# Column sums of Wq by VectorE additions and one product with minus ones, and raw transposed x loaded from tile 2 on

## The reference

```python
h = layernorm(x)
q = rotate(h @ Wq); k = rotate(ctx @ Wk); v = ctx @ Wv
x = x + softmax(q k^T / 4) v @ Wo
h = layernorm(x)
scores = (h @ Wr^T) @ keys^T
gate = softmax over the 16 largest scores, 0 elsewhere
out = x + 2 * ((h @ A^T).reshape(64, 8) * gate).reshape(512) @ B^T
```

## Time and profile before

| | us |
|---|---|
| median of 3 runs | 168.08 (167.92 to 168.69) |
| profiled execution | 168.37 |
| its span in the trace | 166.7 |
| TensorE busy | 160.6 (96%) |
| VectorE busy | 135.0 (81%) |
| ScalarE busy | 95.8 (57%) |
| GpSimd busy | 87.9 (53%) |

### The profile page before, as it was taken

One profiled execution on the slowest core, in us unless ns is written; L12 is line 12 of the kernel. 1 busy time (PEld: TensorE's weight loads), 2 busy tenths in 40 slices (PEclk: granted clock), 3 DMA queues, 4 the chain that ended last, 5 costly groups with the idle time before them and its releaser, 6 DMA issues.

```text
span 166.7 us, 4195 instructions
## 1 busy us (share of the span) xinstructions
PE 160.6 (96%) x1437; PEld 128.9 (77%) x1437; DVE 135.0 (81%) x394; ACT 95.8 (57%) x216; POOL 87.9 (53%) x114
## 2 busy tenths in 40 slices
PE   7899999899999999999999999999999999999993
PEld 2557786777878787879887987979898877779883
DVE  2959895995998899699888998799886997867562
ACT  3588989899657453942678138832487254414210
POOL 6469999899889843724942098106321204411200
PEclk9999999999999999999999999999999999999999
DMA  5999961303315234415442263114410001000013
GB/s 118 403 402 387 409 198 67 132 6 120 98 32 159 49 79 110 117 46 172 114 112 66 93 163 94 49 49 144 109 64 4 4 0 65 0 6 0 0 63 126
DMA packets 12116, 18.45 MB, mean 111 GB/s; under 512 B 2496, under 2 KB 5056, under 8 KB 11840
## 3 DMA queue, kind: packets, MB, share of 16 engines
q1 hardware_dynamic: 11808, 17.93, 34.9%
q10 hardware_dynamic: 288, 0.27, 0.5%
HBM read 11.11 MB, written 2.10 MB: 79 GB/s over the span
## 4 chain that ended last, share of the span: by engine, by line
PE 81%; DVE 9%; issue 3%; DMA 3%; ACT 2%; ACTq 0%; DVEq 0%
PE ps_w L1342 12%; PE ps_w L1343 11%; PE ps_w L1347 11%; PE ps_t L1355 6%; PE ps_s L1426 4%; PE ps_w L1335 3%; PE ps_w L1337 3%; PE ps_w L1336 3%; DVE ps_s L1029 3%; DMA cT_in<-cT 3%; PE ps_t L1496 2%; PE ps_w L1559 2%; PE ps_t L1347 2%; PE ps_t L1343 2%; PE ps_t L1342 2%
## 5 line engine op out<-in xcount | busy, mean ns | idle before, releaser
L483 POOL TENSOR_TENSOR late<-late,gate 128x512 f32<-128x512 f32 x7 | 7.6, 1084 | 31.5 <-issue 15.0
L698 ACT ACTIVATE eT<-ps_s 128x512 f32<-128x512 f32 x32 | 17.0, 601 | 2.5 <-PE ps_s L1485 1.6
L1342 PE MATMUL ps_w<-am_hi,x2T_hi 128*128 128x288 f32 x48 | 13.8, 310 | 0.3 <-ACT x2T_hi L719 0.2
L468 POOL TENSOR_TENSOR oT_lo<-o_n,oT_hi 128x512 fp32r<-128x512 f32 x8 | 10.4, 1294 | 6.6 <-ACT oT_hi L706 6.6
L1343 PE MATMUL ps_w<-am_lo,x2T_hi 128*128 128x288 f32 x48 | 13.1, 296 | 0.0
L1342 PE MATMUL ps_w<-b_hi,zT_hi 128*128 128x512 f32 (+1 forms) x28 | 11.0, 398 | 0.0
L1019 DVE TENSOR_REDUCE ps_s<-ps_s 128x8 f32<-128x512 f32 x16 | 10.6, 688 | 0.3 <-PE ps_s L1426 0.2
L1029 DVE TENSOR_REDUCE ps_s<-ps_s 128x8 f32<-128x512 f32 x16 | 10.4, 692 | 0.5 <-PE ps_s L1445 0.3
L1335 PE MATMUL ps_w<-wq_hi,xT_hi 128*128 128x512 f32 x26 | 10.8, 414 | 0.0
L414 POOL TENSOR_TENSOR rstd<-ve,neg_half 128x1 f32<-128x1 f32 x8 | 4.4, 554 | 11.8 <-DVE ve L947 10.5
L1343 PE MATMUL ps_w<-b_lo,zT_hi 128*128 128x512 f32 (+1 forms) x28 | 10.4, 378 | 0.0
(11 more groups left out here) (280 smaller groups left out, 549.5 us busy)
## 6 DMA issues: line engine op xcount, KB each, us to landing
x_sb<-x SPq DMA_DIRECT2D x8, 256.0 KB, 6.2
q_stack<-qT_hi SPq DMA_DIRECT2D x32, 64.0 KB, 2.0
cT_in<-cT SPq DMA_DIRECT2D x7, 256.0 KB, 3.1
out<-res SPq DMA_DIRECT2D x7, 256.0 KB, 2.3
wq_sb<-wq SPq DMA_DIRECT2D x4, 256.0 KB, 5.1
late<-wo SPq DMA_DIRECT2D x1, 1024.0 KB, 7.5
am_sb<-aT SPq DMA_DIRECT2D x1, 1024.0 KB, 8.3
b_sb<-bT SPq DMA_DIRECT2D x1, 1024.0 KB, 6.7
```

The costliest lines, as they stand in the source:

```text
L468: pool.tensor_tensor(oT_lo[:], o_n[:].rearrange("p (b r q) -> p r b q", b=2, r=REP), oT_hi[:].bitcast(F32), ALU.subtract).then_inc(oT_lo_o ...
L698: act.activation(eT[:, c].rearrange("p b n -> p (b n)"), ps_s[:, c, :], ACT.Exp)\
L1342: pe.matmul(dst, hi(k), w_hi[:, k, cols], start=(k == 0), stop=False)
```

## The change

- DIRECT goes from 4 to 2: tiles 2 and 3 no longer are normalised and turned, their raw x is loaded. `rotate_q(2)` and `rotate_q(3)` get the additional VectorE instruction, and `deviation1(2)` and `deviation1(3)` make a `cs_q`. `x_low(2)` on VectorE reads `xT_raw` in SBUF, not PSUM; `x_low(3)` goes from VectorE to GpSimd.
- The column sums: three VectorE additions over the four chunks of Wq (`add_wq`, into `res`) and one fp32 product of a 128x128 tile of minus ones with the 128x512 result. The four loads, the four ScalarE passes and the four transposes go. `sum_columns` and `sums_out` move from the end of step 1 to `second()`.
- In `first()` on TensorE `kv_high(2)` and `kv_low(2)` stand ahead of and behind `turn_m(0)`; `kv_low(2)` stood behind the turned scores.
- In step 1 `turn_m(2)` stands between the halves of `out_low(1)`, and on VectorE `m_parts(2)`, `k_low(3)` and `residual(1)` stand ahead of `x2_low(0)` and `rotate_q(3)`.
- `statistics1(3)` on VectorE and `deviation1(3)` on GpSimd move to the end of `second()`.

```diff
-DIRECT = 4
+DIRECT = 2
...
-        sums = sb("sums", [P, DK])
+        neg_ones = sb("neg_ones", [P, P])
...
-            return (ps_t1 if t < FIRST else ps_t0)[:, 0:P]
+            return (ps_t1 if t < FIRST - 1 else ps_t0)[:, 0:P]
...
             def load_xT(t):
                 if t == DIRECT:
-                    sp.wait_ge(wq_sum_ok, 1)
+                    sp.wait_ge(q_ps, 1)
                 else:
                     sp.wait_ge(x_lo_ok, t - RAW_Q)
                 sp.dma_start(xT_raw[:], xT[t]).then_inc(ld_xT[t], 16)
...
-            def load_wqT(k):
-                if k == 0:
-                    sp.wait_ge(q_ps, RAW)
-                elif k == 2:
-                    sp.wait_ge(wo_l, REP)
-                sp.dma_start(wqT_of(k), wqT[:, k, :]).then_inc(ld_wqT[k], 16)
...
             load_c(2)
+            load_xT(2)
             sp.dma_start(am_sb[:, :, E:AM], aT).then_inc(ld_am, 16)
...
             load_x(4)
             load_x(5)
-            load_wqT(0)
-            load_wqT(1)
+            load_xT(3)
             load_c(4)
-            load_wqT(2)
-            load_wqT(3)
             load_x(6)
...
                 if t >= DIRECT:
                     pool.wait_ge(rstd1_ok, t + 1)
-                    pool.wait_ge(q_rot, 2 * t)
+                    if t > DIRECT:
+                        pool.wait_ge(q_rot, 2 * t)
                     pool.tensor_scalar(cs_q[:], cs[:, t, :], rstd1[:], None, ALU.mult).then_inc(cs_q_ok, 1)
...
+            pool.memset(neg_ones[:], -1.0).then_inc(ones_ok, 1)
...
             def second():
-                deviation1(3)
                 split_lo(wo_lo, wo_sb, wo_hi, wo_h, wo_l, 1)
...
                 o_low(0)
+                x_low(3)
                 split_lo(am_lo, am_sb, am_hi, am_h, am_l, 1)
                 split_lo(am_lo, am_sb, am_hi, am_h, am_l, 2)
...
                 k_blocks(2, 0)
                 k_blocks(2, 1)
+                deviation1(3)
                 split_lo(am_lo, am_sb, am_hi, am_h, am_l, 3)
...
-                if p >= DIRECT:
+                if p > FIRST:
                     deviation1(p)
...
                     act.wait_ge(ld_xT[t], 16)
                     raw = xT_raw[:]
                 act.activation(xT_hi[:], raw, ACT.Copy).then_inc(x_hi_ok, 1)
...
-            def wq_sum(k):
-                act.wait_ge(ld_wqT[k], 16)
-                act.activation(wqT_of(k), wqT_of(k), ACT.Identity, scale=-1.0, accum_out=sums[:, k:k + 1])\
-                   .then_inc(wq_sum_ok, 1)
...
                 k_high(1)
-                normalise(2)
                 split_hi(wo_hi, wo_sb, wo_h, 1)
...
                 q_high(1)
-                normalise(3)
                 split_hi(am_hi, am_sb, am_h, 0)
...
                 o_high(0)
+                x_high(3)
+                sums_out()
                 value_blocks(2)
                 c_high(3)
                 act.wait_ge(ld_b, 16)
                 split_hi(b_hi, b_sb, b_h, 0)
                 split_hi(b_hi, b_sb, b_h, 1)
-                x_high(3)
                 m_out(1)
                 split_hi(b_hi, b_sb, b_h, 2)
...
                     x2_centre(g)
-                    wq_sum(0)
-                    wq_sum(1)
                 q_high(n)
-                if f < 0:
-                    wq_sum(2)
-                    wq_sum(3)
                 values_out(p)
...
                 m_out(n)
-                if f < 0:
-                    sums_out()
                 x2_centre(i)
...
             def x_low(t):
                 dve.wait_ge(x_hi_ok, t - RAW_Q + 1)
-                dve.tensor_tensor(xT_lo[:], xhT_bank(t)[:].rearrange("p (k q) -> p k q", k=DK),
-                                  xT_hi[:].bitcast(F32), ALU.subtract).then_inc(x_lo_ok, 1)
+                raw = xhT_bank(t)[:].rearrange("p (k q) -> p k q", k=DK) if t < DIRECT else xT_raw[:]
+                dve.tensor_tensor(xT_lo[:], raw, xT_hi[:].bitcast(F32), ALU.subtract).then_inc(x_lo_ok, 1)
+
+            def add_wq(n):
+                for k in (n, n - 1) if n == 1 else (n,):
+                    dve.wait_ge(ld_wq[k], 16)
+                if n > 1:
+                    dve.wait_ge(wq_added, n - 1)
+                dve.tensor_tensor(res[:], wq_sb[:, 0, :] if n == 1 else res[:], wq_sb[:, n, :], ALU.add)\
+                   .then_inc(wq_added, 1)
...
             def result(t):
                 dve.wait_ge(up_ps, t + 1)
                 if t == 0:
-                    dve.wait_ge(wq_sum_ok, 2)
+                    dve.wait_ge(sums_ps, 1)
...
                 rotate_k(0)
                 statistics1(1)
+                add_wq(1)
                 dve.wait_ge(q_ps, 1)
...
                 rotate_q(1)
                 x_low(2)
-                statistics1(3)
 
             def second():
                 rotate_k(2)
+                add_wq(2)
+                add_wq(3)
                 q_low(1)
                 attend(0)
...
                 rotate_q(2)
-                x_low(3)
                 residual(0)
                 statistics2(0)
+                statistics1(3)
...
-                if p >= DIRECT:
+                if p > FIRST:
                     statistics1(p)
...
                 top(n, 1)
-                k_low(p)
                 if f < 0:
                     m_parts(n)
+                    k_low(p)
+                    residual(i)
                     x2_low(g)
                     rotate_q(p)
                 else:
+                    k_low(p)
                     m_parts(n)
                     z_low(f)
-                residual(i)
+                    residual(i)
                 statistics2(i)
                 if f >= 0:
                     result(f)
...
             def sum_columns():
-                pe.wait_ge(wq_sum_ok, DK)
-                for k in range(DK):
-                    mm = pe.transpose(SUMS[:, P * k:P * (k + 1)], sums[:, k:k + 1].broadcast_to([P, P]), ident[:])
-                mm.then_inc(sums_ps, 1)
+                pe.wait_ge(ones_ok, 1)
+                pe.wait_ge(wq_added, DK - 1)
+                pe.matmul(SUMS, neg_ones[:], res[:], start=True, stop=True).then_inc(sums_ps, 1)
...
                 q_low_part(1, [1])
                 project_q(1, [2, 3]).then_inc(q_ps, 1)
-                pe.wait_ge(qT_lo_ok, 1)
-                turn_xh(2)
+                kv_high(2)
                 turn_m(0)
-                kv_high(2)
+                kv_low(2)
...
             def second():
                 pe.wait_ge(sel_ok, 2)
                 turned_scores(0)
-                kv_low(2)
                 pe.wait_ge(q_rot, 4)
                 project_q(2, [0, 1])
                 turn_q(1)
                 values(0)
                 project_q(2, [2])
+                pe.wait_ge(qT_lo_ok, 2)
                 turn_k(2)
                 project_q(2, [3]).then_inc(q_ps, 1)
-                pe.wait_ge(qT_lo_ok, 2)
-                turn_xh(3)
                 scores(1, 0)
                 scores(1, 1)
+                sum_columns()
                 pe.wait_ge(v_st_ok, 3)
                 out_high(0)
...
                 if f < 0:
                     turn_k(p)
                 pe.wait_ge(v_st_ok, p + 1)
-                project_out(i)
+                out_high(i)
                 if f >= 0:
+                    out_low(i)
                     pe.wait_ge(q_rot, 2 * p + 2)
                     up_high(f)
-                turn_m(n)
-                if f >= 0:
+                    turn_m(n)
                     up_low(f)
                     turn_q(p)
                 else:
-                    pe.wait_ge(x2T_lo_ok, i)
-                    sum_columns()
+                    out_low_part(i, [0, 1])
+                    turn_m(n)
+                    out_low_part(i, [2, 3]).then_inc(y_ps, 1)
```

8 lines of the change are left out of this document (2 added, 6 removed).

## The result

The changed kernel takes 169.62 us in the median (169.2 to 169.86), the kernel before 168.09 (167.92 to 168.69) on the same chip: a ratio of 1.0086 [1.0061, 1.011]. It is slower by 0.9%, where 0.6% was forecast. The profiled execution took 169.69 us, its span is 168.0.

The account below looks back on a forecast made before the run. VectorE's chain through attend(2) to tile 3's maxima was taken to bound the kernel: attend(2) 1.4 us late, less 0.42 of slack, adds 1.0 at the end. 168.08 becomes 169.1 us, range 168.6 to 169.6, chance 0.45.

Parts of the forecast that it names:

- TensorE's 1.2 us: TensorE's saving from dropped transposes, old sums and a filled wait, less the new product, if no other engine is late.
- the dear rival: Rival: each two-input SBUF instruction waits for a whole GpSimd operation and GpSimd for it; +1.8, 169.9 us; chance 0.17.
- Start to attend(0): VectorE's opening stretch: three shared-input instructions cost some 0.5 us more each, yet attend(0) starts at 27.1, 0.25 early.
- attend(0) to attend(1): ScalarE copies the sums ahead of m_out(1), which starts at 34.8, 0.5 late; turned scores, exponentials and attend(1) follow, +0.5.
- residual(1) to attend(2), the term that decides: VectorE's stretch in step 1 gets 2.58 us more and loses 0.81 of rest: 9.3 for 7.55, attend(2) 1.4 late.
- it cancels: Rival: shared inputs cost nothing, the gate gives back 0.46, tile 3's turned maxima 0.1 to 0.5 late; 168.3 us; chance 0.26.
- From attend(2) to the turned maxima: m_split(3) ends 1.4 late at 67.15; TensorE turns it at 67.2, +1.0, the 0.42 us of slack being spent.
- The stack's transfers: Transfers into the stack stand behind the selection's, about 2 us later, but have about as much time as before.
- a sign that it is wrong: The prediction is wrong if a transfer (A^T or the stack) ends a wait that no row before shows.
- Costed at nothing: Removed ScalarE passes, 1 MB less to load, and A^T's load with two microseconds of cover: no effect on the time.
- the saving arrives: Rival: TensorE's saving reaches the end, 166.9 us at most, if attend(2) starts at 55.0; chance 0.12.
- The shared inputs cost more: Rival: whole GpSimd operations waited for, attend(0) at 28 and later, residual(1) at 49; 169.9 us (169.6 to 170.5); chance 0.17.

Follow-up runs that it names:

- e4: Changed kernel with the second and third addition of the column sums left out, the product kept (output not the reference's): 169.75 us, ratio 1.0103.
- e3: Changed kernel with ScalarE's copy of tile 1's turned maxima, m_out(1), moved ahead of the first two splits of B: ratio 1.011.
- e1: Changed kernel with x2_low(0) on VectorE moved ahead of residual(1), into the wait there: 168.95 us, ratio 1.0044.
- e2: Changed kernel without the additional VectorE instruction for the mean in rotate_q(3) (output not the reference's): 169.1 us, ratio 1.0049.
- e6: Changed kernel with tile 2's attention reciprocals in another PSUM bank, so scores(3)'s second half need not wait for attend(2)'s products: 169.88 us, ratio 1.0103.
- p2: Kernel before with the new column sums alone, two of the additions in the rest ahead of attend(1): 168.95 us, ratio 1.0039.
- v4: Changed kernel with seven moves, among them x2_low(0) ahead of residual(1), tile 4's statistics early, B's splits behind tile 1's exponentials: 168.69, then 168.49 us.

## Why the prediction was right, and where it was off

The direction, the place and the mechanism were right: TensorE's 1.2 us don't arrive, attend(2) is late, nothing gives that back, and it ends at the stacked products. The size was +1.0 and is +1.5. The median, 169.62, lies at the upper edge of the forecast's own range (168.6 to 169.6) and within that of the dear rival (169.6 to 170.5). Of the two profiled executions the changed kernel's starts 0.35 us earlier, which hid part of the miss: that attend(2) at 57.61 and the end of m_split(3) at 67.17 meet the forecast of 57.6 and 67.15 is luck, for from `q_b(0)` on attend(2) is 1.77 late and not 1.4. From `q_b(0)` on, with what the sum said:

| step | before | changed | difference | forecast |
|---|---|---|---|---|
| attend(0) | 15.26 | 15.31 | +0.05 | -0.25 |
| attend(1) | 27.25 | 28.18 | +0.93 | +0.5 |
| residual(1) | 36.55 | 36.71 | +0.16 | -0.39 |
| attend(2) | 44.10 | 45.87 | +1.77 | +1.4 |
| turned maxima of tile 3 | 54.08 | 55.78 | +1.70 | +1.0 |
| next product | 57.18 | 59.04 | +1.86 | +1.0 |

So 0.86 us are missing from `q_b(0)` on. Step by step they are 0.30 up to attend(0), 0.13 to attend(1), 0.12 to residual(1), -0.18 to attend(2), 0.33 to the turned maxima and 0.16 to the next product.

**Start to attend(0), mis-sized by 0.3.** The price of the shared inputs was nearly right, 1.33, 1.07 and 0.93 us for a forecast of 1.1 each. From start to start x_low(2) took 1.26, and the two additions 2.44 with a rest of 0.51 between them, 3.70 together for 3.4; the rotation between them took 0.08 less, and x_low(2) began 0.08 later. e4 shows that even without the additions ScalarE allows only 0.2.

GpSimd is held up by more than the 0.3 that was taken for each of four instructions. GpSimd in order of time:

```profile
10.48 1.23 POOL L392 TENSOR_TENSOR wkv_lo<-wkv_sb,wkv_hi 128x256 fp32r<-128x256 f32 x1
...
21.77 1.04 POOL L447 TENSOR_TENSOR k_bd_hi<-kT_hi,half_mask 128x512 fp32r<-128x512 f32 x1
22.77 1.75 POOL L427 TENSOR_TENSOR q_r<-q_a,q_b 128x512 f32<-128x512 f32 x1
24.49 1.48 POOL L447 TENSOR_TENSOR k_bd_lo<-kT_lo,half_mask 128x512 fp32r<-128x512 f32 x1
25.93 4.24 POOL L392 TENSOR_TENSOR wo_lo<-late,wo_hi 128x512 fp32r<-128x512 f32 x3
...
45.44 1.31 POOL L456 TENSOR_TENSOR oT_lo<-o_n,oT_hi 128x512 fp32r<-128x512 f32 x1
```

q_r takes 1.30 elsewhere, k_bd_lo 1.04, the three wo_lo took 3.79: 0.45 more each time. wkv_lo, which took 0.73 before, was held up 0.50 by the first addition. That addition had begun 0.05 ahead of it, at 10.43, and took its plain 0.69. And VectorE's lengths follow: x_low(2) began at 22.03 and ended at 23.36, 0.59 behind the end of k_bd_hi; the additions, begun at 24.01 and 25.59, ended 0.59 behind 24.49 and 25.93. Each waited until the GpSimd operation that was running had ended, and then took its own 0.6. By this the rest of 0.51 between the two additions cost nothing: k_bd_lo ran until 25.93, and the third addition could not end before 26.52 wherever it began.

The Trainium skill's rule (SBUF — State Buffer, section "Who interferes with whom") says this, and the trace agrees: the price for VectorE is the remainder of the running GpSimd operation, 0.74, 0.48 and 0.34 us here. That GpSimd is held up in turn, which no row before showed, is now shown too.

oT_lo(1) ended at 46.75, for a forecast of 46.5; from `q_b(0)` on it is 0.6 later than forecast, as the four delays make 1.8 us and not 1.2.

**attend(0) to attend(1).** m_out(1) came at 34.86 for a forecast of 34.8, 7.81 us behind attend(0) where it was 6.91. This term was right, ScalarE's copy of the sums ahead of it and all. (Two slips of its working do not matter: 30.5 + 0.92 is 31.4 and not 31.55 for the end of the product, and 0.43 and 0.25 are three quarters of 0.92, not half.) e3 shows that the order was not at fault but the amount.

**residual(1) to attend(2), the term that decides.** 9.16 us, forecast 9.3. Right; e1 and e2 show it from two sides. The gate still meets b_lo and takes 0.72 us, so that what the rival "it cancels" counted on did not come.

**From attend(2) to the turned maxima, the step that failed.** The prediction took 0.42 us between the end of the split maxima and their turning for slack of TensorE, and said that "TensorE's own list is not later than that". m_split(3) ended at 67.17, forecast 67.15, and TensorE turned it at 67.52, again 0.35 later. Those 0.35 to 0.42 are TensorE's list behind the turning of k(4), which hangs on attend(2) as the maxima do (e6). A distance between two engines is slack only if what fills it doesn't hang on the same event. This is 0.33 of the missing 0.86, the largest single part.

**The stack's transfers** were said to have "about as much time as before". By the list of issues that was right, 0.5 us to spare before and 0.3 after. But the last one landed 0.5 late, and TensorE's wait of 0.27 for it cost 0.16. The prediction had named such a wait as a sign that it is wrong, and the sign came; the prediction had no term for the time to landing.

**Costed at nothing.** A^T's load and the removed passes of ScalarE showed no wait, as forecast. Of the rivals, "it cancels" and "the saving arrives" fall with attend(2) at 57.61. "The shared inputs cost more" had the mechanism, and the median in its range, but the price of its additions fell into a rest (e4), and attend(0) came at 27.05, not at 28. How much x_low(2)'s part of it costs is open.

What stays open, besides: why the third addition began 0.51 us behind the end of the second, when no other row of the changed kernel up to 80 us lists such a wait of VectorE for itself; in p2, where the same two stand alone, no such rest is listed.

## What to carry to other kernels

Work taken from the busiest engine is worth nothing if another engine's chain starts each stage: look for the one instruction all roads lead through (here attend(2)), and price what a change puts ahead of it. Before a gap between two engines is counted as slack, follow what fills it back to its own releaser. And when one cause is mended, look for the next one at the same instruction: v4 took VectorE's added work from ahead of attend(2), and this then hung on ScalarE's high part of x2(1) again, as it did at the start, level with it.

## What the runs showed of the hardware

SyncE's issues of 0.59 us were now and then 0.4 to 1.2 us longer (1.43 in the changed kernel, 1.58 in e6, 1.31 in v4, 1.78 in e4). Between 50 and 78 us each of the thirteen traces has exactly two issues of 0.97 us or more in the lists for the stack and the output, and exactly two packets of instructions on DMA queue 8, 16 KB each, and each of these 26 packets stands within 0.7 us of the start of such an issue (changed kernel: packets at 60.4 and 74.4, issues at 60.69 and 74.75; kernel before: 55.0 and 72.8, issues at 55.40 and 73.20). So a long issue comes with a load of instructions; that SyncE waits for the next piece of its program is the plain reading, and no run tested it.

In one execution of v4 TensorE ran at half its pace from the first product on, and the whole took 310 us, though the granted clock is shown as 1.00 in every stretch and TensorE was busy for 99% of the span. No row says why. Its first eight products of q, 3.67 us in the earlier trace rows:

```profile
10.10 7.72 PE L1552 MATMUL ps_w<-wq_sb,xT_raw 128*128 128x512 f32 x8
```

The row of warming products ahead of it looked like any other's (4.28 us for 9, 4.02 in e6). It was seen once and is in no ratio here.
